# The turn from the last attention layer to the mixture of experts: weights asked for earlier, the last chunk routed in halves, the tile table laid over partitions

## The reference, cut to what matters

```python
def _L3_ffn_ref(x, keys, w1, b1, w2, b2, rw, rb):
    E, TOP_K = (16, 4)
    diff = x[:, :, None, :] - keys
    dist2 = jnp.sum(diff * diff, axis=-1)
    logits = -dist2 + jnp.einsum('bld,ed->ble', x, rw) + rb
    topv, topi = jax.lax.top_k(logits, TOP_K)
    w = jax.nn.softmax(topv, axis=-1)
    hidden = jax.nn.gelu(jnp.einsum('bld,efd->blef', x, w1) + b1, approximate=False)
    exp_out = jnp.einsum('blef,edf->bled', hidden, w2) + b2
    sel = jnp.take_along_axis(exp_out, topi[..., None], axis=2)
    return jnp.sum(w[..., None] * sel, axis=2)
x = x + jnp.tanh(g_xattn[3]) * _L3_xattn_ref(_layernorm(x), ctx_1024, ...)   # 16 heads of 64
x = x + jnp.tanh(g_ffn[3]) * _L3_ffn_ref(_layernorm(x), ...)
```

## Time and profile before

| | us |
|---|---|
| runs before | 1720.52 median of 3 (1719.59 to 1722.77) |
| the profiled execution's own time | 1724.73 |
| its span, first to last instruction | 1722.9 |
| PE busy | 1431.9 |
| DVE busy | 1158.2 |
| ACT busy | 1039.6 |
| POOL busy | 525.3 |

### The profile page before, as it was taken

How to read it: one execution, slowest core, us unless ns; L and a number is a source line. 1 busy time by engine, 2 the same in 40 slices (tenths; PEclk the granted TensorE clock), 3 DMA queues, 4 the chain that set the end, 5 groups by cost and what they waited for, 6 DMA issues and landing times.

```text
span 1722.9 us, 35704 instructions
## 1 busy us (share of the span) xinstructions
PE 1431.9 (83%) x9952; PEld 1032.1 (60%) x9956; DVE 1158.2 (67%) x3748; ACT 1039.6 (60%) x3072; POOL 525.3 (30%) x552
## 2 busy tenths in 40 slices
PE   3776777799769979799699999999987239999995
PEld 2554555466644436344366666666666139999995
DVE  2788888588657666587257687677667536666665
ACT  2677878455445546222477777777776227777663
POOL 4354338122111102200000223322323345555451
PEclk9899999799989999899899999999999569999998
DMA  8000009900189911000000000000000612222227
GB/s 184 14 12 6 6 7 178 135 0 0 31 143 179 179 25 43 7 1 0 7 1 8 25 16 27 27 20 18 26 15 19 239 51 68 64 65 69 61 63 244
DMA packets 143562, 98.43 MB, mean 57 GB/s; under 512 B 20610, under 2 KB 132652, under 8 KB 142292
## 3 DMA queue, kind: packets, MB, share of 16 engines
q1 hardware_dynamic: 134740, 80.15, 23.1%
q0 software_dynamic: 8704, 16.87, 3.0%
HBM read 43.10 MB, written 54.93 MB: 57 GB/s over the span
## 4 chain that ended last, share of the span: by engine, by line
PE 41%; issue 33%; DVE 9%; ACT 9%; POOL 3%; another core or an unknown queue 2%; DMA 2%; SPq 1%; DVEq 0%; ACTq 0%; POOLq 0%
PE bank L924 7%; PE bank L1338 6%; PE bank L1330 6%; PE bank L940 4%; ACT att L1494 3%; PE bank L973 3%; ACT arena L1371 3%; PE bank L960 2%; PE bank L928 2%; PE bank L950 2%; DVE nm L1856 2%; DVE att L1857 1%; ACT att L1771 1%; PE bank L866 1%
## 5 line engine op out<-in xcount | busy, mean ns | idle before, releaser
L1371 ACT ACTIVATE arena<-bank 128x512 f32<-128x512 f32 (+6 forms) x460 | 261.6, 601 | 146.6 <-PE bank L1259 55.4
L556 POOL TENSOR_TENSOR rstd<-ve,mhalf 128x4 f32<-128x4 f32 x64 | 64.8, 1012 | 485.6 <-DVE ve L1837 485.6
L1771 ACT ACTIVATE att<-bank,arena 128x128 f32<-128x128 f32 x576 | 164.5, 370 | 67.7 <-PE bank L1330 64.4
L700 POOL DMA_INDIRECT dispatched_rows<-arena x128 | 129.4, 1011 | 212.8 <-DVE arena L1918 141.0
L1494 ACT ACTIVATE att<-bank,arena 128x128 f32<-128x128 f32 x512 | 180.3, 395 | 18.1 <-DVE arena L2000 15.5
L751 POOL DMA_INDIRECT expert_outputs<-arena x144 | 144.3, 1002 | 147.4 <-issue 102.2
L1338 PE MATMUL bank<-arena,att 128*128 128x128 f32 x1152 | 153.7, 276 | 1.5 <-ACT att L1771 1.0
L1330 PE MATMUL bank<-xnT,arena 128*128 128x128 f32 x1152 | 153.7, 277 | 0.3 <-ACT xnT L1371 0.2
L1338 PEld LDWEIGHTS bank<-arena,att 128*128 128x128 f32 x1152 | 140.1, 192 | 4.1 <-ACT att L1771 4.0
L1330 PEld LDWEIGHTS bank<-xnT,arena 128*128 128x128 f32 x1152 | 141.3, 193 | 0.9 <-ACT xnT L1371 0.9
L1371 ACT ACTIVATE xnT<-bank 128x128 f32<-128x128 f32 (+1 forms) x180 | 63.4, 352 | 119.9 <-PE bank L772 49.5
(11 more groups left out here) (349 smaller groups left out, 3239.6 us busy)
## 6 DMA issues: line engine op xcount, KB each, us to landing
dispatched_rows<-padf SPq DMA_DIRECT2D x16, 2128.5 KB, 31.9
arena<-dispatched_rows SPq DMA_DIRECT2D x144, 64.5 KB
cxT<-in_ctx SPq DMA_DIRECT2D x32, 256.0 KB
arena<-in_L_ffn_w SPq DMA_DIRECT2D x8, 1024.0 KB
arena<-expert_outputs SPq DMA_DIRECT2D x8, 1024.0 KB, 14.3
expert_outputs<-arena POOLq DMA_INDIRECT x144
dispatched_rows<-arena POOLq DMA_INDIRECT x128
out_x<-x SPq DMA_DIRECT2D x8, 256.0 KB, 4.3
```

The costliest lines, as they stand in the source:

```text
L700: pl.indirect_dma_start(sent, bass.IndirectOffsetOnAxis(di3[:, q:q + 1], 0), rows3[:, q, :], None)\
L1371: copy = lambda o, i: nc.scalar.activation(o, i, ACT.Copy)
L1771: last = nc.scalar.activation(h3[:, s % 2, k * P:k * P + P], bank[s % 2][:, k * P:k * P + P], ACT.Gelu, bias=b1c3[:, s % 4, k:k + 1])
```

## The change

Three things change, all at the turn.

1. SyncE no longer waits for stage F3. It asks for the first weights once the scores of chunk 6 are done, for the second once those of chunk 7 are done, and for the biases once the last probabilities are transposed.
2. Routing. Chunk 6 is routed in steps 2 to 6 of chunk 7 and not in 2 to 7, in bank 5. Chunk 7's residual and routing are done in halves of two sequences. Half 0 gets residual and statistics in step 7 and the rest in the drain, in bank 6; half 1 follows, in bank 5. They have a row buffer of their own (`last3`, `last_places`), so they don't wait for chunk 6's rows to be gone. POOL sends 4 of chunk 6's 16 groups of 128 rows, takes half 0's inverse deviation, sends 12, takes half 1's, then sends 8 and 8. In all routings the places are now worked out before the shares.
3. The tile table has an expert on each of 16 partitions; the sums over experts are three products on PE. The iota of tile numbers moves to POOL's start.

```diff
-            stage_start(sp, STAGE["F3"])
             s_w = sem("F3_weights_loaded")
+            sp.wait_ge(sem("A3_scores"), (NC - 1) * (2 * PAIRS))
             for e in range(0, E3, EL3):
                 sp.dma_start(w1T3[:, e:e + EL3, :], a["L3_ffn_w1"][:, e:e + EL3, :]).then_inc(s_w, 16)
+            sp.wait_ge(sem("A3_scores"), NC * (2 * PAIRS))
+            for e in range(0, E3, EL3):
                 sp.dma_start(w2T3[:, e:e + EL3, :], a["L3_ffn_w2"][:, e:e + EL3, :]).then_inc(s_w, 16)
+            sp.wait_ge(sem("A3_pT_full"), NC * (2 * PAIRS))
...
-            dispatch(NC - 2)
-            stage_start(pl, STAGE["F3"])
-            pl.iota(iota3[:, :], pattern=[[1, NT]], base=0, channel_multiplier=0, allow_small_or_imprecise_dtypes=True)\
-                .then_inc(sem("F3_constants"), 1)
+            rows_complete(NC - 2)
+            send(range(SC // 4))
             inverse_deviation(NC - 1)
-            dispatch(NC - 1)
+            send(range(SC // 4, SC))
+            inverse_deviation(NC)
+            for half in range(2):
+                rows_complete(NC - 1 + half)
+                send(range(half * SC // 2, (half + 1) * SC // 2), half)
...
                     if j == 2:
                         reach(pe, "F3_rows_ready", c, 1, 0)
+                        if isinstance(c, int) and c == NC - 1:
+                            pe.wait_ge(sem("A3_half_read"), 1)
...
+                        if live and not more and w in (3, 4, 5):
+                            routing(c - 1, {3: 8, 4: 9, 5: 12}[w])
+                        if not live:
+                            routing(c - 1, {0: 8, 1: 9, 2: 12}[w], 0)
...
+                def residual_half(c, half):
+                    js = HALVES[half]
+                    at, of = slice(js[0] * P, (js[-1] + 1) * P), slice(js[0], js[-1] + 1)
+                    dve.wait_ge(sem("A3_y"), c * CB + js[-1] + 1)
+                    step(v.tensor_tensor(tmp[:, of, :], bank[7][:, at].rearrange("p (j d) -> p j d", j=len(js)),
+                                         bo3[:, :].unsqueeze(1).to_broadcast([P, len(js), P]), ALU.add))
+                    dve.sem_inc(sem("A3_half_read"), 1)
+                    last = v.scalar_tensor_tensor(xc(c)[:, of, :], tmp[:, of, :], gate3[:, 0:1], xc(c)[:, of, :], ALU.mult, ALU.add)
...
+                        if live and not more:
+                            for u in {2: (6,), 3: (7, 8), 5: (9, 10), 6: (12,)}.get(w, ()):
+                                routing(c - 1, u)
+                            if w == 7:
+                                residual_half(c, 0)
+                                routing(c, 6, 0)
+                        if not live:
+                            if w < 2:
+                                values(c, w - 2)
+                            for u in {0: (7, 8), 1: (9, 10)}.get(w, ()):
+                                routing(c - 1, u, 0)
+                            if w == 2:
+                                residual_half(c - 1, 1)
+                                routing(c, 6, 1)
+                                routing(c - 1, 12, 0)
+                            continue
...
-            step(v.tensor_tensor(until3[:, :, :], cum3[0:1, n, :].unsqueeze(1).to_broadcast([1, NT, E3]),
-                                 iota3[:, :].unsqueeze(2).to_broadcast([1, NT, E3]), ALU.is_le))
-            step(v.tensor_reduce(tabf3[:, 0, :], until3[:, :, :], AX, ALU.add))
+            step(v.tensor_scalar(rank3[:, :], iota3[:, :], tiles3[:, 0:1], None, ALU.subtract))
+            v.tensor_scalar(until3[:, :], rank3[:, :], before3[:, 0:1], None, ALU.is_ge).then_inc(sem("F3_tiles_reached"), 1)
```

More of the change, by code:

```diff
@@ L352, in flamingo, with route_bank, rows_of, qs_of @@
         flat_wv3, flat_wo3 = wv3[:, :].rearrange("p (q t) -> p q t", t=P), wo3[:, :, :]
+        ALL = tuple(range(CB))
+        HALVES = ((0, 1), (2, 3))
+        def route_bank(c, half):
+            if half is not None:
+                return bank[6 - half]
+            return bank[5 if isinstance(c, int) and c == NC - 2 else 7]
+        def rows_of(half):
+            return (rows3, rowsu3, di3) if half is None else (last3, lastu3, lastdi3)
+        def qs_of(js):
+            return slice(js[0] * TOP3, (js[-1] + 1) * TOP3)
         def diagonal(i, q):
@@ L696, in rows_complete, with send @@
                 pl.sem_inc(s_held, 1)
-            def send(qs):
+            def send(qs, half=None):
+                held, _, places = rows_of(half)
                 for q in qs:
-                    pl.indirect_dma_start(sent, bass.IndirectOffsetOnAxis(di3[:, q:q + 1], 0), rows3[:, q, :], None)\
+                    pl.indirect_dma_start(sent, bass.IndirectOffsetOnAxis(places[:, q:q + 1], 0), held[:, q, :], None)\
                         .then_inc(sem("F3_dispatched"), 16)
@@ L705, in rows_sent @@
                 pl.sem_inc(sem("F3_rows_free"), 1)
-            def dispatch(c):
-                rows_complete(c)
-                send(range(SC))
-                rows_sent(c)
             def dispatch_beside(c, ahead):
@@ L773, in transpose_x, with routing @@
                 return last
-            def routing(c, u):
+            def routing(c, u, half=None):
+                js, at = ALL if half is None else HALVES[half], route_bank(c, half)
+                n = len(js) * E3
                 if u == 8:
                     pe.wait_ge(sem("F3_normalised"), c + 1)
-                    for j in range(CB):
-                        last = nc.tensor.transpose(bank[7][:, j * P:j * P + P], xr3[:, j, :], ident[:, :])
+                    for j in js:
+                        last = nc.tensor.transpose(at[:, j * P:j * P + P], xr3[:, j, :], ident[:, :])
                     last.then_inc(sem("F3_routing"), 1)
@@ L784, in routing @@
                     pe.wait_ge(sem("F3_xnT"), c + 1)
-                    for j in range(CB):
-                        last = nc.tensor.matmul(bank[7][:, 2 * P + j * E3:2 * P + j * E3 + E3], xrT3[:, j * P:j * P + P], wr3[:, :], start=True, stop=True)
+                    for i, j in enumerate(js):
+                        last = nc.tensor.matmul(at[:, 2 * P + i * E3:2 * P + i * E3 + E3], xrT3[:, j * P:j * P + P], wr3[:, :], start=True, stop=True)
                     last.then_inc(sem("F3_routing"), 1)
@@ L1512, in body @@
                             piece(c + 1, 1 - p, s)
-                        if live and not first and w in (3, 5, 6):
+                        if live and not first and more and w in (3, 5, 6):
                             routing(c - 1, {3: 8, 5: 9, 6: 10}[w])
+                        if live and not more:
+                            for u in {3: (8,), 5: (9, 10)}.get(w, ()):
+                                routing(c - 1, u)
+                        if not live:
+                            for u in {0: (8,), 1: (9,), 2: (10,)}[w]:
+                                routing(c - 1, u, 0)
                         for side in range(2):
@@ L1869, in routing @@
                     dve.wait_ge(sem("F3_rows_copied"), c + 1)
-                    for j in range(CB):
-                        last = v.tensor_scalar(xr3[:, j, :], xc(c)[:, j, :], mv[:, j, 0:1], rstd[:, j:j + 1], ALU.subtract, ALU.mult)
+                    for j in js:
+                        last = v.tensor_scalar(xr3[:, j, :], xc(chunk)[:, j, :], mv[:, j, 0:1], rstd[:, j:j + 1], ALU.subtract, ALU.mult)
                     last.then_inc(sem("F3_normalised"), 1)
@@ L1920, in heads0 @@
+                    step(v.reciprocal(es3[:, of], es3[:, of]))
+                    step(v.tensor_scalar(es3[:, of], es3[:, of], gates[:, 7:8], None, ALU.mult))
+                    kept = wt3[:, bass.ds(c * SC, SC)] if half is None else wt3[:, chunk * SC + qs.start:chunk * SC + qs.stop]
+                    step(v.tensor_tensor(kept.rearrange("p (j k) -> p j k", j=n), ex3[:, of, :],
+                                         es3[:, of].unsqueeze(2).to_broadcast([P, n, TOP3]), ALU.mult))
             def heads0():
@@ L2031, in residual @@
                     v.scalar_tensor_tensor(xc(c), tmp[:, :, :], gate3[:, 0:1], xc(c), ALU.mult, ALU.add).then_inc(s_xdone, 1)
+                def residual_half(c, half):
[6 more added lines that the diff above has]
+                    last = v.scalar_tensor_tensor(xc(c)[:, of, :], tmp[:, of, :], gate3[:, 0:1], xc(c)[:, of, :], ALU.mult, ALU.add)
+                    if half:
+                        last.then_inc(s_xdone, 1)
+                    else:
+                        step(last)
                 def body(c, p, more, first=False, live=True, ahead=True):
```

170 lines of the change are left out of this document (97 added, 73 removed).

## The result

The changed kernel takes 1704.3 us (median of 4 runs, 1701.29 to 1704.7) against 1720.94 before (4 runs, 1719.59 to 1722.77): a ratio of 0.9899, 95% interval 0.9882 to 0.9916, so 17.4 us or 1.0% faster (14.5 to 20.3). Two repeats gave 0.9894 (0.9877 to 0.9910) and, on another chip, 0.9906 (0.9889 to 0.9922). The forecast was 1705.5, in a range of 1694 to 1713. The profiled execution took 1701.29 us for a span of 1699.5. So the single traces must be read stretch by stretch.

A forecast was written before the change was run, and what follows sets the result against it. POOL's sends, held behind weights, were taken to end PE's wait at the turn. First tile load 13 us earlier with news late, 17 on time; middle 15: 1720.5 - 15 = 1705.5 us, range 1694 to 1713.

The forecast's parts named there:

- held case: At the turn: sends wait while weights flow; 13 us gained with news late, 17 on time; chance 0.49, range 1702 to 1709.
- hold: POOL's sends wait until expert weights have passed; read from 6.89 us idle between chunk 7's first two sends.
- late news: Others learn late of PE's finished work while POOL sends: half-products 4.0 us, projection 5.4 us late before.
- a send meets it: held until 1336.3: In the drain, one of chunk 6's first four sends meets w2, putting last half-products at 1343, not 1339.
- second reading: DVE's two-input operations of 2304 elements, not weights, caused the idle time between chunk 7's first two sends.
- free case: Rival at the turn: sends not held; 22 us gained, 27 with news on time (best end), 1693.5 to 1698.5; chance 0.35.
- half 1's routing: After half 1's residual: residual to places takes 11.4 us plus 2 of late news, against 17.2 before.
- rival with more in the way: Half 1's three handovers from PE each 4 us late, outlasting half 0's sends: 7 us off, 1712.5; chance 0.10.
- step order on PE: Chunk 7's steps 5 to 7: earlier routing delays step 7's maxima 3.4 us, block 2's projection 1.8 us net.
- weights early: Expert weights asked for during chunk 7's steps rather than at F3; not on the path, worth nothing by itself.
- Table on partitions: Tile table after the places shrinks from 14.0 us to about 5; worth nothing, since POOL's sends cover it.

The follow-up runs named there:

- weights late: Changed kernel with all expert-weight loads put back to the start of F3; ratio to before 0.9916, first chip.
- sends late: Changed kernel, but POOL takes both inverse deviations ahead of chunk 6's other twelve sends; ratio to before 0.9914, first chip.
- weights only: Kernel before, with only SyncE's early asking for expert weights; ratio to before 0.9966, second chip.
- order only: Kernel before, with places worked out ahead of shares in every routing; ratio to before 0.9998 on the second chip, 0.9989 on the third.
- shifted: Changed kernel with twelve idle POOL instructions ahead of chunk 6's first send; ratio to before 0.9882, second chip.
- half 0 ahead: Changed kernel with half 0's logits, choice and places moved forward in the drain; ratio to before 0.9864, second chip.
- six sends more: Chunk 5's first six groups sent twice, third chip: ratio to before 0.9916 in the changed kernel, 0.9897 in half 0 ahead.

## Why the forecast came out right, point by point

The time, 1704.3 for 1705.5, lies in the held case's own range, but the mechanism that I gave that case is not what happened. That they meet is luck: a hold that wasn't there was made up for by late news in a place where I had none, and by a pause that I took for a hold. From chunk 7's first maxima on (1277.55 before, 1269.34 after), in us:

| | before | forecast, held (free) | after |
|---|---|---|---|
| first send of chunk 6 | 51.2 | 46.7 | 48.2 |
| last half-products start | 57.8 | 65.5 (61.5) | 65.8 |
| chunk 6's twelve sends end | | 76.5 (68.5) | 70.0 |
| residual (of half 1) | 72.8 | 71.5 to 80.5 | 76.9 |
| half 0's first send | | 85.2 (76.0) | 81.6 |
| places of half 1 done | 89.9 | | 90.3 |
| table written | 104.0 | | 96.7 |
| first tile load | 121.3 | 106.3 (99.1) | 107.1 |

- **Failed: "a send meets it: held until 1336.3".** Sends pass beside full DMA engines (weights late). The idle 6.89 us of the earlier trace rows was a pause of 3.1, stretched while weights flowed (7.43 in weights late, with DVE's two-input operations gone). The second reading, DVE's two-input operations, explained the send of 2.41 us, as the prediction said, and nothing of the idle time.
- **Right: news is late while POOL sends.** Sends late shows it, and that it costs 10 us of path. It fell elsewhere than I had it. ACT's late copy ahead of the last half-products (3.3 us), which I left out, put them where the hold had put them. Their own news was 4.6 us late for 4.0 before, but the projection's, 5.4 late before, was on time, since the sends had ended at 1339.38. So the residual too came inside the held case's stretch, and half 0's first send 3.6 us ahead of it; the pause of 3.1 then took that back. With no hold and news on time the load would have come at 94.5 (the free case's best end). The second chip shows 95.9, with the 3.1 of the pause in it, which that case left out. (The free case's load, 1376.6, is 0.2 more than its own terms add up to; nothing hangs on it.)
- **Right: half 1's routing.** Residual to places takes 13.4 us, as the 11.4 and 2 of the sum; the 2 of late news weren't there, the chain was as much longer, so that its sum fits is luck as well. The rival with more in the way did not come: even in sends late, with a run of sends all through, half 1's handovers are on time.
- **Half right: step order on PE.** Step 7's maxima come 50.4 us behind the first ones and were forecast at 48.9, the projection of block 2 at 54.5 for 52.9: 1.6 us more lost. PE waits 3.87 us for DVE's choice and then runs transposes and scores in 1.92 and 2.08 us (granted clock 0.62 from 1308 to 1315), where before they took 1.09 and 1.16 at 1.00 in the same step; the forecast took the latter.
- **Missed: the pause stays.** 3.1 us of it are in the changed kernel, where the forecast had it gone with the weights.
- **Missed: weights early, "worth nothing by itself".** Taking that part back costs 4.2 us of turn (weights late), and it gives 3.7 alone (weights only).
- **Missed: "Table on partitions", "Worth nothing".** 2.8 us, by two sends that were slowed, not by its length.
- **Missed: the bodies.** 5.75 us in the traces, part of which the medians show: the turn's 14.2 and the measured 17.4 (14.5 to 20.3) leave 0.3 to 6.

Of the turn's 14.2 us, 4.2 are then the weights' and 2.8 the table's. The 7.2 that are left belong to the halves and POOL's new order, by subtraction only: no run has them alone. On the second chip the turn is 20.6 shorter than in order only, and less the weights' 3.7 and the 1.4 that the slowed send still costs weights only, some 15 are left. This is an estimate from single traces; by it, routing in halves is worth more where news is on time.

**Open** is what the pause is. It stands between the 113th and the 114th indirect DMA in every trace without the six sends, is 3.1 to 3.6 us, and 6.6 to 7.4 while weights flow. It is no effect of weights (weights only), of a run's start (sends late), of the place in the program (shifted), nor of POOL standing still (half 0 ahead), nor of the number of DMAs issued (six sends more, where it doesn't show).

## What to carry to other kernels

Price a collision by a row in which both sides run side by side for long, not by a single gap: one idle 6.9 us beside full DMA engines looked like a hold and wasn't. Where one engine waits for news while another sends, look at what the sends are for: those of chunk 6 were on nobody's path while they cost the drain 10 us, and they could only be moved at the price of the next ones. An operation that is hidden by its length may still slow the one that hides it.

## What the runs showed of the hardware

The waits that answer to the earlier trace rows, in the changed kernel (us, times, longest):

```profile
DVE arena L2071 <- remote: 51.1, 12, 10.7
```

- PE's semaphore news is late while POOL issues indirect DMAs on two of the three chips (51.1, 50.9 and 49.9 us of such waits before DVE's copies, 12 each, in three traces of the changed kernel) and never on the second, on which before takes 1703.1 us. Sends late shows the link; why the second chip is free of it, no run tells. Half 1's handovers were on time in the middle of sends; why, no run tells either.
- A send that begins 0.59 us or more behind the start of a DVE operation with two inputs of 2304 elements (2.55 us) ends 0.84 or 0.85 us behind that operation's end: seven sends of 1.55 to 2.79 us for 0.96, in five traces. One that began 0.02 us behind the start was not slowed.
- Indirect sends are issued every 1.26 us beside weights at 415 GB/s, but the last one's landing was waited for 5.45 us there (order only) for 1.58 (weights only).
- PE at its lower clock: sixteen half-products take 1.97 us for 1.09, a projection 3.78 for 2.05 (changed kernel, sends late).
- A pause of 3.1 us ahead of the 114th indirect DMA, and one of 3.5 ahead of the 242nd, in the tile loop, where nobody waits for it; with six sends more the first is gone and the second stands ahead of the 248th.
